# A tile's own features move into the half bank and to VectorE, and two deepest ranks share a slot

## The reference

```
scores = where(mask, -arange(N), -inf);  vals, idx = top_k(scores, 25)
agg = x[idx] (or -inf where not valid), max over the 25
agg = where(degree <= 25, maximum(agg, 0), agg)
out = relu(concat([x, agg], -1) @ W + b)
x = layernorm(x + out)
```

## Time and profile before

| what | value |
|---|---|
| runs (3) | 729.66, 733.22, 740.46 us; median 733.22 |
| profiled execution | 733.26 us, its span 731.6 us |
| busy: VectorE, TensorE (matmuls), ScalarE, GpSimd | 602.6, 546.3, 452.1, 293.0 us |
| granted TensorE clock, mean | 0.934 |
| instructions | 13267 |

### The profile page before, as it was taken

The page is one execution under the profiler, slowest core; times in us unless marked ns, Lnnn a source line. Parts: engine busy times, 40 slices in busy tenths (PEclk is TensorE's granted clock), DMA queues, the critical chain, the costliest instruction groups (busy, mean ns, idle before and its releaser), DMA issues.

```text
span 731.6 us, 13267 instructions
## 1 busy us (share of the span) xinstructions
PE 546.3 (75%) x3837; PEld 318.1 (43%) x3888; DVE 602.6 (82%) x1004; ACT 452.1 (62%) x855; POOL 293.0 (40%) x430
## 2 busy tenths in 40 slices
PE   3668878787877877877868877777767788786963
PEld 2435444444444434444434444444434444442532
DVE  5778899889897789977878778987789878995984
ACT  6825774568755687556855577746686567642544
POOL 3622643344235333445323453334523444244510
PEclk9799999999998999998989899999999989997996
DMA  6521222322043122412133121322113310011102
GB/s 240 188 77 48 84 71 77 93 80 77 30 134 95 49 78 77 127 58 82 49 91 112 56 84 51 122 81 88 52 63 107 109 62 20 3 52 34 34 6 58
DMA packets 32679, 56.65 MB, mean 77 GB/s; under 512 B 4515, under 2 KB 21158, under 8 KB 32550
## 3 DMA queue, kind: packets, MB, share of 16 engines
q1 hardware_dynamic: 26150, 42.08, 17.5%
q0 software_dynamic: 6400, 13.12, 6.1%
HBM read 50.99 MB, written 4.19 MB: 75 GB/s over the span
## 4 chain that ended last, share of the span: by engine, by line
PE 31%; DVE 30%; issue 16%; ACT 9%; DVEq 7%; another core or an unknown queue 5%; DMA 1%; ACTq 0%; POOL 0%; SPq 0%; POOLq 0%
PE pair L1008 22%; DVE part L745 14%; DVE hot L740 4%; DVE g_feat L818 3%; PE half L1008 3%; DVEq L815 2%; ACT distance L592 2%; ACT hot L584 2%; DVE g_val L786 2%; PE p_maskT L982 2%; DVE g_score L788 1%; DVEq L877 1%; ACT row_work L673 1%; DMA adj_sb<-in_adj 1%
## 5 line engine op out<-in xcount | busy, mean ns | idle before, releaser
L1008 PE MATMUL pair<-hot,x_part 128*128 128x512 bf16 (+2 forms) x1608 | 383.7, 377 | 109.6 <-DVE part L745 78.2
L745 DVE TENSOR_REDUCE part<-pair 128x128 f32<-128x1024 f32 x256 | 310.9, 1220 | 95.8 <-PE pair L1008 70.8
L1008 PEld LDWEIGHTS pair<-hot,x_part 128*128 128x128 bf16 x1608 | 148.0, 101 | 263.8 <-DVE part L745 78.8
L453 POOL DMA_INDIRECT g_feat<-in_x,g_idx x200 | 192.3, 962 | 121.2 <-issue 93.9
L490 POOL TENSOR_TENSOR y_sb<-relu_sb,x_sb 128x128 f32<-128x128 f32 x64 | 35.8, 560 | 295.7 <-ACT relu_sb L610 295.5
L565 ACT ACTIVATE V<-p_V 128x512 bf16<-128x512 f32 x98 | 58.0, 592 | 93.2 <-remote 68.3
L610 ACT ACTIVATE relu_sb<-misc 128x128 f32<-128x128 f32 x64 | 17.6, 275 | 116.3 <-PE misc L1065 79.0
L740 DVE TENSOR_SCALAR hot<-V 128x1024 bf16<-128x1024 bf16 x224 | 82.1, 376 | 0.0
L584 ACT ACTIVATE hot<-V,first_bias 128x1024 bf16<-128x1024 bf16 x56 | 63.8, 1139 | 21.8 <-PE pair L1008 18.8
L599 ACT ACTIVATE hot<-distance,one 128x1024 bf16<-128x1024 bf16 x56 | 64.2, 1146 | 0.0
L592 ACT ACTIVATE distance<-V,second_bias 128x1024 bf16<-128x1024 bf16 x56 | 63.6, 1136 | 0.0
(11 more groups left out here) (93 smaller groups left out, 607.8 us busy)
## 6 DMA issues: line engine op xcount, KB each, us to landing
adj_sb<-in_adj SPq DMA_DIRECT2D x56, 512.0 KB
g_adj<-in_adj SPq DMA_DIRECT2D x8, 512.0 KB
x_sb<-in_x SPq DMA_DIRECT2D x8, 512.0 KB
out<-y_sb SPq DMA_DIRECT2D x7, 512.0 KB
g_feat<-in_x,g_idx POOLq DMA_INDIRECT x200
out<-y_sb SPq DMA_DIRECT2D x1, 448.0 KB
w_sb<-in_W SPq DMA_DIRECT2D x1, 128.0 KB, 7.0
out<-y_sb SPq DMA_DIRECT2D x1, 64.0 KB
```

Source lines behind the costliest of these rows:

```text
L453: pool.indirect_dma_start(out=g_feat[w][:, k, :], out_offset=None, in_=x_rows, in_offset=bass.IndirectOffsetOnAxis(ap=g_idx[w][:, k:k + 1] ...
L745: dve.tensor_reduce(part[:, par(q, s), :, p], slots_of(s, p)[:, :, :].rearrange("f k i -> f i k"), AX.X, ALU.max).then_inc(s_used, 1)
L1008: last = pe.matmul(dst, x_part[:, q, part_no, kb], one_hot, start=(part_no == 0), stop=(part_no == PARTS - 1))
```

## The change

- The half bank's fourth slot takes the tile's own features (`turn_features` at the head of group 3). VectorE copies them into xt_sb as part of `reduce_group`, and then reduces the first three slots. `transpose_x`, its waits and ScalarE's copy are gone.
- That leaves two slots fewer for ranks in the half group, one of them the slot in which the deepest rank of block 0 and that of block 1 are now summed (`shared`). Where a node has both, the sum is wrong, so a tile with such a node is redone (`reached`, a further column of `viol`: `VIOLS`).
- Blocks 0 and 1 each lose a rank from the other banks, so that the pieces fall differently: three matmuls more in steps 1, 2 and 3, the same number in steps 4 to 7.
- The features of tile 0 are turned ahead of group 3 of step 5 rather than at its end; p_V's waits change with it.
- ScalarE: relu of tile 0 moves from the end of step 7 to the next step 1, behind first_rank and second_distance, and that of tile 7 behind them in step 2; second_rank, make_mask, x0_t, agg0_t and the pieces of means, squares and deviation come ahead of the second half of V, and the relu of the tile before comes behind it.

```
-    filled = banks(depths)
+    shared = [(kb, depths[kb] - 1) for kb in range(2)]
+    filled = banks([d - (kb < 2) for kb, d in enumerate(depths)])
+    filled[-1] += [(kb, r, 1, BANK - 2) for kb, r in shared]
...
+    VIOLS = NT + 2
...
     assert FRONT == MT
-    assert all(sum(piece[2] for piece in group) == (BANK if p == HALF_PLACE else 2 * BANK)
-               for s in GROUPS for p, group in enumerate(GROUPS[s]))
+    assert all({place + k for kb, r, n, place in group for k in range(n)}
+               == set(range(BANK - 1 if p == HALF_PLACE else 2 * BANK)) for s in GROUPS for p, group in enumerate(GROUPS[s]))
...
         hotx = sb("hotx", [P, DEEPER, NT, P], BF16)
-        viol = sb("viol", [P, LEVELS, MT, NT + 1], BF16)
+        viol = sb("viol", [P, LEVELS, MT, VIOLS], BF16)
+        reached = sb("reached", [P, MT, 2], F32)
...
                     to_rank, to_turn, to_mask = (ahead(i, q, s, FRONT + k) for k in range(3))
-                    if s == 2 and not is_first(i, q):
-                        relu(pi, pq, MT)
...
                         second_distance(*nxt)
+                    if s == 1 and not is_first(i, q):
+                        relu(pi, pq, 0)
+                    if s == 2 and not is_first(i, q):
+                        relu(pi, pq, MT)
...
                         copy_maskT(*to_turn)
-                    act.wait_ge(s_xt, m + 1)
-                    if not (isinstance(m, int) and m < 2):
-                        act.wait_ge(s_out, m - 1)
-                    nc.scalar.activation(xt_sb[:, par(q, s)], p_xt, ACT.Copy).then_inc(s_xtc, 1)
...
                         second_rank(*nxt)
-                    if s > 1:
-                        relu(i, q, s - 1)
-                    if s == MT:
-                        act.wait_ge(s_agg0t, 2 * i + q + 1)
-                        nc.scalar.activation(agg0_t[:, :], p_xt, ACT.Copy).then_inc(s_agg0c, 1)
-                    if to_rank:
-                        copy_V(*to_rank, 1)
...
                         nc.scalar.activation(x0_t[:, :], p_xt, ACT.Copy).then_inc(s_x0c, 1)
+                    if s == MT:
+                        act.wait_ge(s_agg0t, 2 * i + q + 1)
+                        nc.scalar.activation(agg0_t[:, :], p_xt, ACT.Copy).then_inc(s_agg0c, 1)
...
                             deviation(before, pq)
-                        if s in (6, 7):
-                            normalise(before, pq, range(4 * (s - 6), 4 * (s - 5)))
+                    if to_rank:
+                        copy_V(*to_rank, 1)
+                    if s > 1:
+                        relu(i, q, s - 1)
+                    if s in (6, 7) and not is_first(i, q):
+                        normalise(2 * i + q - 1, pq, range(4 * (s - 6), 4 * (s - 5)))
...
                         split_mid(ni, nq)
-                    if s == MT:
-                        relu(i, q, 0)
...
+            relu(B // 2 - 1, 1, 0)
...
                 dve.wait_ge(s_pair, pair_no(i, q, s, p) + 1)
-                dve.tensor_reduce(part[:, par(q, s), :, p], slots_of(s, p)[:, :, :].rearrange("f k i -> f i k"),
+                slots = slots_of(s, p)
+                if p == HALF_PLACE:
+                    m = pos(i, q, s)
+                    if not (isinstance(m, int) and m < 2):
+                        dve.wait_ge(s_out, m - 1)
+                    dve.tensor_copy(xt_sb[:, par(q, s)], slots[:, BANK - 1]).then_inc(s_xtc, 1)
+                    slots = slots[:, 0:BANK - 1]
+                dve.tensor_reduce(part[:, par(q, s), :, p], slots[:, :, :].rearrange("f k i -> f i k"),
...
                     dve.tensor_tensor(viol[:, lv, :, 0:NT], cnt[:, 0], depth_tab[:, lv], ALU.is_gt)
+                dve.tensor_tensor(reached[:, :, :], cnt[:, 0, :, 0:2], depth_tab[:, 0, :, 0:2], ALU.is_ge)
...
                 dve.drain()
+                dve.tensor_tensor(viol[:, 1, :, NT + 1], reached[:, :, 0], reached[:, :, 1], ALU.mult)
...
                 dve.wait_ge(s_vp, 2 * i + q + 1)
-                dve.tensor_reduce(vsum[:, :, :], p_viol.rearrange("p (l t b) -> p l t b", l=LEVELS, b=NT + 1),
+                dve.tensor_reduce(vsum[:, :, :], p_viol.rearrange("p (l t b) -> p l t b", l=LEVELS, b=VIOLS),
...
+            dve.memset(viol[:, 0, :, NT + 1], 0.0)
...
-            def pick(dst, q, kb, one_hot, signal=None):
+            def pick(dst, q, kb, one_hot, signal=None, first=True, final=True):
                 for part_no in range(PARTS):
-                    last = pe.matmul(dst, x_part[:, q, part_no, kb], one_hot, start=(part_no == 0),
-                                     stop=(part_no == PARTS - 1))
+                    last = pe.matmul(dst, x_part[:, q, part_no, kb], one_hot, start=(first and part_no == 0),
+                                     stop=(final and part_no == PARTS - 1))
...
                     pe.wait_ge(s_used, pair_no(i, q, s, p) - since_last_use(s, p) + 1)
+                if p == HALF_PLACE:
+                    turn_features(q, s, half[:, BANK - 1])
                 pieces = GROUPS[s][p]
-                for kb, r, n, place in pieces:
+                for k, (kb, r, n, place) in enumerate(pieces):
                     one_hot = hot[:, u, r:r + n, kb] if r < LOW else hot_high[:, u, r - LOW:r - LOW + n, kb]
-                    pick(slots_of(s, p)[:, place:place + n], q, kb, one_hot,
-                         s_pair if (kb, r, n, place) == pieces[-1] else None)
+                    pick(slots_of(s, p)[:, place:place + n], q, kb, one_hot, s_pair if k == len(pieces) - 1 else None,
+                         first=k == 0 or pieces[k - 1][3] != place,
+                         final=k == len(pieces) - 1 or pieces[k + 1][3] != place)
...
-            def turn_features(q, t, signal):
+            def turn_features(q, t, dst, signal=None):
                 for part_no in range(PARTS):
-                    last = pe.matmul(p_xt, x_part[:, q, part_no, t], ident_bf[:, :], start=(part_no == 0),
+                    last = pe.matmul(dst, x_part[:, q, part_no, t], ident_bf[:, :], start=(part_no == 0),
                                      stop=(part_no == PARTS - 1))
-                last.then_inc(signal, 1)
-            def transpose_x(i, q, s):
-                m = pos(i, q, s)
-                ranked = ahead(i, q, s, FRONT)
-                if not (isinstance(m, int) and m == 0):
-                    pe.wait_ge(s_xtc, m)
-                pe.wait_ge(s_V, 2 * pos(*ranked) + 1 if ranked else 2 * MAIN)
-                if s == 1 and not is_first(i, q):
-                    pe.wait_ge(s_agg0c, 2 * i + q)
-                if s == 6:
-                    pe.wait_ge(s_x0c, 2 * i + q + 1)
-                turn_features(q, s, s_xt)
+                if signal is not None:
+                    last.then_inc(signal, 1)
...
                     if to_rank:
-                        if s == 6:
-                            pe.wait_ge(s_x0c, 2 * i + q + 1)
...
                     pick_group(i, q, s, 1)
-                    transpose_x(i, q, s)
...
                         linear_main(i, q, s - 1)
-                    pe.wait_ge(s_xtc, m + 1)
+                    if s in (5, MT):
+                        pe.wait_ge(s_V, copied - 1 if to_rank else copied)
+                    if s == 5:
+                        turn_features(q, 0, p_xt, s_x0t)
                     if s == MT:
+                        pe.wait_ge(s_x0c, 2 * i + q + 1)
...
                     pick_group(i, q, s, 3)
+                    if s == 5:
+                        pe.wait_ge(s_x0c, 2 * i + q + 1)
...
                         pe.nop(nofuse=True)
-                    if s == 5:
-                        pe.wait_ge(s_V, copied)
-                        turn_features(q, 0, s_x0t)
...
                             pe.wait_ge(s_V, copied)
-                            if s == 5:
-                                pe.wait_ge(s_x0c, 2 * i + q + 1)
...
                     with pe.Else():
```

More of the change, by code:

```diff
@@ L199, in build @@
         p_cnt = misc[:, P:P + MT * NT]
-        NV = LEVELS * MT * (NT + 1)
+        NV = LEVELS * MT * VIOLS
         p_viol = misc[0:1, 2 * P:2 * P + NV]
@@ L233, in build @@
         s_agg = sem("agg_ready")
-        s_xt = sem("x_transposed")
         s_xtc = sem("xT_ready")
```

## The result

| | kernel before | changed kernel | ratio, 95% interval |
|---|---|---|---|
| time, us | 734.23 (729.66 to 740.46, 4 runs) | 705.25 (704.35 to 705.63, 4 runs) | 0.960 [0.953, 0.967] |
| profiled execution, span | 733.26, 731.6 | 705.23, 703.6 | |

28 us less between the two profiled executions (29 between the medians) where 12 were forecast. 705 lies under the range of 708 to 738.

What follows compares the result with a forecast made beforehand. It took the hand-over of picked-feature groups between VectorE and TensorE to bound the kernel. Terms of -15.0, -3.4, +1.0, +3.7 and +1.6 summed to -12.1 us, from 733 to 721 us, range 708 to 738.

Steps and rivals of the forecast that it cites:

- the prediction's sum: Whole kernel: -15.0 - 3.4 + 1.0 + 3.7 + 1.6 = -12.1 us, giving 721 us; chance 0.47.
- part 5: ScalarE's order: the moved copies, relu and second half of V cost or gain nothing; zero.
- part 1: Third groups, steps 2 to 6: TensorE's mid-step wait for V goes, 15.0 us gained; remaining signal lateness stays.
- part 3: VectorE's own-feature copies: 284 ns each, net 66 ns 56 times, 3.7 us lost; count_violations adds 1.6 us.
- The price that I rejected: Step 4's own-feature pause taken at its TensorE row's 3.41 us: 24 us over seven batches, against under 5.
- Part 2: Tile 0's features in step 5: the wait for V's other half at the step's end goes, 3.4 us gained.
- The new wait at x0: Step 5: second rank product waits for ScalarE's x0 copy; 1 us in all, 8 if 1 us a batch is uncovered.
- Part 4: Shared slot: three more matmuls in steps 1 to 3, no tile added to the full redo; 0, at most 4 us.
- Rival A: Clock stays up at step 4's own-feature product: 12 us on top of the sum, 709 to 711 us; chance 0.23.
- a sign against its sum: Step 4: the prediction would be wrong if the low-clock stretches there went.
- B: Rival: freed waits reappear at the next late signal and copies cost more; 732 us, or 738; chance 0.23.
- C: Rival: V's second half comes late for the first rank product of steps 3 to 6; 749 us; chance 0.07.

Runs made afterwards that it cites:

- after_relu_early: Changed kernel with the relu of the tile before back behind second_rank, ahead of V's second half: 720.4 us, 1.014 of the kernel before (717.0).
- before_gathers_step4: Kernel before with only step 4's gathers held until the last group but two of step 3 is reduced: 653.0 us, ratio 1.000 (signals on time).
- before_no_runs: Kernel before with gathers in parts of two or one and step 4's x_rest ahead of its single gather: 658.9 us, ratio 1.009 (signals on time).
- after_no_runs: Changed kernel with gathers in parts of two or one and x_rest earlier: 655.8 us, 1.003 of the kernel before (signals on time).
- before_relu_late: Kernel before with the relu of the tile before moved behind V's second half, the new mask and the layernorm pieces: 711.4 us, ratio 0.997.
- before_gathers_split: Kernel before with a step's five gathers in parts of two, two and one, behind reductions of groups 0, 2 and 4: 675.7 us, ratio 0.943.
- before_gathers_unbroken: Kernel before with each step's five gathers in one run after its first group's reduction: 659.6 us, ratio 1.009 (signals on time).
- unbroken_again: Kernel before with each step's five gathers in one run after its first reduction, in a session with late signals: 788.2 us, ratio 1.079.
- before_split_clear: Kernel before with gathers in pairs and step 4's x_rest ahead of the third part: 660.6 us, ratio 1.010 (signals on time).

## Why the prediction was wrong

The parts are those of the prediction's sum. In VectorE's waits and work it was short by 15.6 us: 8.2 at part 5, 3.7 at part 1, 3.6 at part 3, the rest small.

**Two steps failed: the reading of the late signals in part 1, and with it part 5, "Zero".** Part 1 said that the lateness "has nothing to do with ScalarE", that the real pause in step 4 was 0.65 us of a row's 3.41, and that TensorE's rows end too early. They end where they should. V's signal itself was late, so ScalarE's copy was, and TensorE's wait of 2.9 us for it was real. The lateness is no fixed property of TensorE's signals either: it follows GpSimd's gathers, and these follow ScalarE's relu.

*Part 5, ScalarE's order, "Zero", is the term that was missed.* 8.2 us at step 4's first group, and the interplay with step 2 (22 us between `after_relu_early` and after). I asked what waits for the relu and named only the count; GpSimd's residual waits for it too, more than for anything else, and behind that in GpSimd's program stand the gathers, which I never laid beside the late signals. The list of waits of the kernel before had it:

```profile
POOL y_sb L490 <- ACT relu_sb L610: 295.5, 54, 12.8
```

*The size of part 1 came out near all the same, by luck.* The smaller of pause and VectorE wait was summed to 14.0 us for the third groups of steps 3 to 6; they fell by 17.7. The price that I rejected, "24 us over seven batches", would have been worse: step 4's third groups gave 5.4. Step 2 was to keep its wait: it did (27.0 to 25.8), now at the half group, 2.89 us in the fifth batch. But this is a price of the session: without late signals the third groups of steps 3 to 6 wait 2.2 us in all (`before_gathers_step4`), and the whole part is worth no more than that.

*Part 2, tile 0's features.* Forecast 3.4; step 6's first group fell by 3.8 us. This too exists only with late signals: without them the first groups of step 6 wait 0.40 us in all in `before_no_runs` and 0.14 in `after_no_runs`. Step 6 is shorter there by 2.5 us over the eight batches, but 1.6 of it is the wait of one third group, that of the second batch, which part 1 had named. The new wait at x0 did not show.

*Part 3, VectorE's copies.* 284 ns forecast, 284 measured; the half reduction 551 forecast, 547 measured. VectorE's work grew by 1.7 us, and by 2.8 in the pair with no runs, where 5.3 were forecast. Sizes right, sum somewhat too high. The estimate of 258 ns by the Trainium skill ("VectorE: DVE Perf Modes", section "The TRN2 errata") was too low.

*Part 4, the shared slot.* No sign of a cost.

Rival A (the clock) came nearest, 709 to 711, and what it named at step 4 did happen: the six matmuls of the third group took 2.7 us in five batches before and take 1.46 in all eight now, 6.3 us less, and the mean granted clock rose from 0.934 to 0.946. The prediction had called that a sign against its sum. But `before_relu_late` has 1.46 in all eight as well, and its third groups still wait 30.7 us; so the clock goes with the pauses and does not remove them by itself. Which share of the 28 us came by it, no run separates. B and C did not come.

What the runs show, then: with late signals the change gives 28, 15 and 28 us in three sessions; with 24 of 25 gathers left out nothing (1.002), with the gathers split 4.5 us lost, and in sessions without late signals 3 to 4 gained, always with a schedule of gathers that is not the changed kernel's. The changed kernel itself never ran in a session without late signals. So nearly all of its gain exists only with late signals, which its edits make less costly; that they do it by letting TensorE go on inside a step and by starting the gathers later is the reading that fits the waits. That shifting the gathers alone would give part of it was tried three times and never shown; the tables of the relu show it only together with the edits.

## What to carry to other kernels

Where a wait has no cause among its own engines' rows, lay every other engine's rows beside it, GpSimd's above all, and look for what ends when the signals come; one bucket of "lateness" is a theory not made yet. In this kernel indirect gathers in runs of four or more did the harm: two at a time, mostly, and tied to a consumer's progress, they cost about 1% where the signals were on time and gained 6 to 7% where they were late. When an instruction is moved, follow the chain of who waits for it through each engine's queue to the DMAs. And take the kernel before again in every session: here it was 654 or 717 to 734 us with the same program.

## What the hardware did that I had not expected

- TensorE's semaphore increments come late, by 4.4 us at the half group above (due 437.14, seen 441.5), during runs of four or five indirect gathers of GpSimd, and mostly together, 1.1 to 1.4 us behind the last one's end: in the kernel before 123 of the 213 signals due during such a run are over 0.8 us late. Pairs with about 1.1 us between them do much less of it: in `before_gathers_split` 15 of 206, and 13 of 55 during single gathers.
- It comes and goes by session: late in four (kernel before 734, 717, 718, 733), not in two (653.6, 653.8), with the same program; the number of gathers, their 0.95 us each and their bytes are the same in both. What decides it stays open; no run here tells.
- A VectorE one-hot of 1024 bf16 columns that starts with GpSimd's eight subtractions takes 2.98 us instead of 0.42 (`before_gathers_split`), and one that starts 1.66 us into them 1.35 (`before_gathers_unbroken`). Most of those of 128 or 256 columns that start within them take 0.5 at most, but not all: 1.25 to 1.57 us six times in `unbroken_again`, and 2.94 once in `before_split_clear`, where it started 0.16 us ahead of them.
